# Two graph attention layers on one core: the turned probability blocks are stored and sent by query tile instead of by halves of the query quarters

## The reference

```python
h = relu(layernorm(x))
# layer 0
scores = q @ k.T / sqrt(32) + beta * adj
scores = where(adj > 0, scores, -9e15)
x = x + softmax(scores) @ v
h = relu(layernorm(x))
# layer 1
scores = q @ k.T / sqrt(384) + (adj + adj)
scores = where(any(scores != 0, axis=-1), scores, -inf)
x = x + (nan_to_num(softmax(scores)) @ v) @ Wo.T + bo
```

## Time and profile before

| what | value |
|---|---|
| median of 3 runs | 2229.5 us (2227.84 to 2229.7) |
| the profiled execution, its own time | 2227.39 us |
| its span in the profile | 2225.6 us |
| TensorE matmul busy | 1990.9 us, 89% |
| VectorE busy | 1865.0 us, 84% |
| ScalarE busy | 1643.7 us, 74% |
| GpSimd busy | 1072.6 us, 48% |
| DMA packets of the hardware queue (SyncE's) | 61.1% of 16 engines' span |
| DMA packets of the software queue (GpSimd's) | 20.6% |

### The profile page before, as it was taken

How to read it: one execution, slowest core, us unless ns; L and a number is a source line. 1 busy time by engine, 2 the same in 40 slices (tenths; PEclk the granted TensorE clock), 3 DMA queues, 4 the chain that set the end, 5 groups by cost and what they waited for, 6 DMA issues and landing times.

```text
span 2225.6 us, 52690 instructions
## 1 busy us (share of the span) xinstructions
PE 1990.9 (89%) x19584; PEld 1285.9 (58%) x19584; DVE 1865.0 (84%) x4056; ACT 1643.7 (74%) x4151; POOL 1072.6 (48%) x1541
## 2 busy tenths in 40 slices
PE   2899999999999999994499999999999999999984
PEld 1565555656555555552366666666666666666652
DVE  1999999999999999992388888888898888898881
ACT  2898888888888888882387777777777777777761
POOL 5566565565665666521433444443453434443421
PEclk8899999999999999997699999999999999999997
DMA  4688999898988888886477898888898888988784
GB/s 97 131 203 205 211 228 219 215 220 208 216 211 211 213 217 204 207 193 149 111 179 168 185 210 186 186 181 198 186 208 187 181 194 186 208 190 188 164 184 97
DMA packets 114511, 419.28 MB, mean 188 GB/s; under 512 B 35408, under 2 KB 38480, under 8 KB 114256
## 3 DMA queue, kind: packets, MB, share of 16 engines
q1 hardware_dynamic: 77392, 306.81, 61.1%
q0 software_dynamic: 36864, 109.09, 20.6%
HBM read 88.61 MB, written 25.17 MB: 51 GB/s over the span
## 4 chain that ended last, share of the span: by engine, by line
PE 35%; DVE 7%; ACT 5%; DMA 2%; issue 1%; SPq 1%; POOL 1%; DVEq 0%; POOLq 0%
PE ring L258 9%; PE sc L236 7%; PE ring L282 6%; PE out L309 6%; DVE s L374 4%; PE ring L263 3%; ACT s L503 3%; DVE pt L388 2%; PE ring L249 2%; ACT pl L521 1%; PE ring L273 1%; SPq L210 1%; DMA pk<-pt 1%; DMA bob<-in_bo 1%; PE ring L268 1%
## 5 line engine op out<-in xcount | busy, mean ns | idle before, releaser
L503 ACT ACTIVATE s<-s,nmax 128x512 f32<-128x512 f32 x1536 | 1093.6, 724 | 265.7 <-DVE nmax L374 265.2
L374 DVE CUSTOM_DVE_ANT_0 s<-sc,bias 128x512 f32<-128x512 f32 x1536 | 968.5, 686 | 123.6 <-PE sc L236 77.4
L388 DVE STREAM_TRANSPOSE pt<-s 128x2048 f32<-128x2048 f32 x288 | 663.9, 2305 | 6.3 <-issue 6.1
L236 PE MATMUL sc<-k,q 32*128 32x512 f32 x3072 | 450.0, 655 | 81.5 <-DVE nmax L374 77.6
L659 POOL TENSOR_TENSOR v<-v,bvb 128x384 f32<-128x384 f32 x128 | 130.3, 1018 | 539.4 <-ACT v L541 539.0
L309 PE MATMUL out<-pk,v 128*32 128x192 f32 x6144 | 305.8, 342 | 55.2 <-DMA pk<-pt 55.0
L503 ACT ACTIVATION_READ_ACCUMULATOR s<-s,nmax 128x1 f32 x1536 | 308.7, 201 | 0.0
L309 PEld LDWEIGHTS out<-pk,v 128*32 128x32 f32 x6144 | 186.3, 113 | 207.6 <-issue 92.3
L236 PEld LDWEIGHTS sc<-k,q 32*128 32x128 f32 x3072 | 124.6, 187 | 197.7 <-DVE nmax L374 122.3
L258 PE MATMUL ring<-hT,wq 128*128 128x512 f32 x864 | 235.8, 418 | 3.0 <-DVE hT L400 3.0
L263 PE MATMUL ring<-wv,hT 128*128 128x384 f32 x1152 | 236.4, 350 | 0.0
(11 more groups left out here) (79 smaller groups left out, 2042.0 us busy)
## 6 DMA issues: line engine op xcount, KB each, us to landing
pk<-pt SPq DMA_DIRECT2D x1536, 192.0 KB, 6.0
bias<-in_adj POOLq DMA_DIRECT2D x128, 192.0 KB, 6.5
xin<-in_x POOLq DMA_DIRECT2D x64, 192.0 KB, 6.4
res<-in_x POOLq DMA_DIRECT2D x64, 192.0 KB, 9.3
x_between<-res POOLq DMA_DIRECT2D x64, 192.0 KB, 6.6
xin<-x_between POOLq DMA_DIRECT2D x64, 192.0 KB, 6.7
res<-x_between POOLq DMA_DIRECT2D x64, 192.0 KB, 5.5
out_x<-res POOLq DMA_DIRECT2D x64, 192.0 KB, 5.4
```

Of the source, the lines that this page charges most:

```text
L236: mm = nc.tensor.matmul(m.sc[:, j, :], m.q[rows, at, P * t:P * (t + 1)], by_number(k) if t < TURNS else k, start=True, stop=True)
L374: nc.vector.tensor_tensor_reduce(out=m.s[:, t % 2, :, j, :], in0=m.sc[:, j, :].rearrange("p (n e) -> p n e", e=P), in1=m.bias[par][:, t, : ...
L388: nc.vector.transpose(out=to, in_=m.s[:, t % 2].rearrange("p a j (i e) -> p (a j i) e", e=HD)).then_inc(turned, 1)
L503: nc.scalar.activation(tile, tile, ACT.Exp, bias=m.nmax[at][:, t, j:j + 1], scale=-1.0, accum_out=m.sums[at][:, t, j:j + 1]).then_inc(exp_ ...
```

## The change

The two halves are no longer bands of partitions but sets of query tiles: `GROUPS = ((0, 1), (2,))`. `pt` and `pk` become one tensor for each group. `move` sends group 0 (tiles 0 and 1) after the second turn of the step and group 1 (tile 2) after the third. Each group has its own 16 DMAs, of 4096 bytes a partition (128 KB) in group 0 and of 2048 bytes (64 KB) in group 1. So a step has 32 DMAs in place of 16, with the same bytes. Part 1 of `pv` reads group 0 (256 columns a matmul in place of 192) and part 2 reads group 1 (128 columns). The place of each part on TensorE stays.

```diff
-HALVES = 2
-PARTS = 1 + HALVES
+GROUPS = ((0, 1), (2,))
+PARTS = 1 + len(GROUPS)
...
-        moved = [[sem(f"moved_{c}_{half}") for half in range(HALVES)] for c in range(DT)]
+        moved = [[sem(f"moved_{c}_{n}") for n in range(len(GROUPS))] for c in range(DT)]
...
-        LOADS, ADJ, MOVES = 16 * QUADS, 32 * QUADS, 16 * QUADS * QUADS // HALVES
+        LOADS, ADJ, MOVES = 16 * QUADS, 32 * QUADS, 16 * QUADS * QUADS
...
                 s = DT * b + c
-                sp.wait_ge(turned, TURNS * (s + 1))
-                for a in range(QUADS):
-                    half = a * HALVES // QUADS
-                    if a * HALVES % QUADS == 0 and not (part == "first" and c == 0):
-                        sp.wait_ge(pv_ready, PARTS * (s - 1) + half + 2)
-                    for to in range(QUADS):
-                        sp.dma_start(m.pk[HD * to:HD * (to + 1), a], m.pt[HD * a:HD * (a + 1), slab(par, c), to]).then_inc(moved[c][half], 16)
+                for n, tiles in enumerate(GROUPS):
+                    sp.wait_ge(turned, TURNS * s + tiles[-1] + 1)
+                    if not (part == "first" and c == 0):
+                        sp.wait_ge(pv_ready, PARTS * (s - 1) + n + 2)
+                    for a in range(QUADS):
+                        for to in range(QUADS):
+                            sp.dma_start(m.pk[n][HD * to:HD * (to + 1), a], m.pt[n][HD * a:HD * (a + 1), slab(par, c), to]).then_inc(moved[c][n], 16)
...
-                    quads = slice(QUADS // HALVES * (part - 1), QUADS // HALVES * part)
+                    tiles, pk = GROUPS[part - 1], m.pk[part - 1]
...
-                            to = to.rearrange("p (t a e) -> p t a e", a=QUADS, e=HD)[:, 0:TURNS, quads]
-                            p = m.pk[:, quads, j].rearrange("p a (i t e) -> p i t a e", i=QUADS, e=HD)[:, n]
+                            to = to.rearrange("p (t a e) -> p t a e", a=QUADS, e=HD)[:, tiles[0]:tiles[-1] + 1]
+                            p = pk[:, :, j].rearrange("p a (i t e) -> p i t a e", i=QUADS, e=HD)[:, n]
...
-                to = m.pt[:, slab(par, c)].rearrange("p a j (i t e) -> p (a j i) t e", i=QUADS, e=HD)[:, :, t, :]
+                n = [t in tiles for tiles in GROUPS].index(True)
+                to = m.pt[n][:, slab(par, c)].rearrange("p a j (i t e) -> p (a j i) t e", i=QUADS, e=HD)[:, :, t - GROUPS[n][0], :]
...
-        self.pt = sb("pt", [P, 2, QUADS, HC, QUADS * TURNS * HD])
-        self.pk, self.pl = sb("pk", [P, QUADS, HC, QUADS * TURNS * HD]), sb("pl", [P, HC, N])
+        self.pt = [sb(f"pt{n}", [P, 2, QUADS, HC, QUADS * len(tiles) * HD]) for n, tiles in enumerate(GROUPS)]
+        self.pk = [sb(f"pk{n}", [P, QUADS, HC, QUADS * len(tiles) * HD]) for n, tiles in enumerate(GROUPS)]
+        self.pl = sb("pl", [P, HC, N])
```

More of the change, by code:

```diff
@@ L345, in _ @@
                 if kind == "post" and i == 0:
-                    pv(B, -1, DT - 2, HALVES, B % 2, False)
+                    pv(B, -1, DT - 2, len(GROUPS), B % 2, False)
                     for n in range(PARTS):
@@ L383, in turn @@
                     d2, a2 = chunk_ahead(c, -2)
-                    for half in range(HALVES):
-                        dve.wait_ge(moved[a2][half], MOVES * (b + d2 + 1))
+                    for n in range(len(GROUPS)):
+                        dve.wait_ge(moved[a2][n], MOVES * (b + d2 + 1))
                 dve.wait_ge(exp_done, UNITS * s + HC * (t + 1))
-                to = m.pt[:, slab(par, c)].rearrange("p a j (i t e) -> p (a j i) t e", i=QUADS, e=HD)[:, :, t, :]
+                n = [t in tiles for tiles in GROUPS].index(True)
+                to = m.pt[n][:, slab(par, c)].rearrange("p a j (i t e) -> p (a j i) t e", i=QUADS, e=HD)[:, :, t - GROUPS[n][0], :]
                 nc.vector.transpose(out=to, in_=m.s[:, t % 2].rearrange("p a j (i e) -> p (a j i) e", e=HD)).then_inc(turned, 1)
@@ L831, in __init__ @@
         self.s = sb("s", [P, 2, QUADS, HC, P])
-        self.pt = sb("pt", [P, 2, QUADS, HC, QUADS * TURNS * HD])
-        self.pk, self.pl = sb("pk", [P, QUADS, HC, QUADS * TURNS * HD]), sb("pl", [P, HC, N])
-        self.wraw = [self.pt[:, 0, i].rearrange("p a (b n) -> p (a b) n", b=1)[:, 0:DT, :] for i in range(3)]
+        self.pt = [sb(f"pt{n}", [P, 2, QUADS, HC, QUADS * len(tiles) * HD]) for n, tiles in enumerate(GROUPS)]
+        self.pk = [sb(f"pk{n}", [P, QUADS, HC, QUADS * len(tiles) * HD]) for n, tiles in enumerate(GROUPS)]
+        self.pl = sb("pl", [P, HC, N])
+        self.wraw = [self.pt[0][:, 0].rearrange("p a j n -> p (a j n)")[:, DT * D * i:DT * D * (i + 1)].rearrange("p (t n) -> p t n", t=DT) for i in range(3)]
         self.nmax = [sb(f"nmax{i}", [P, NT, HC]) for i in range(2)]
```

## The result

The changed kernel takes 2405.18 us (median of 4 runs, 2397.41 to 2408.16), the kernel before 2228.67 us (its median has 4 runs here): ratio 1.0787, with a 95% interval of 1.076 to 1.0815. The ratios come from all the runs of both kernels, so they can differ a little from the quotient of two medians. The profiled execution of the changed kernel took 2406.66 us at a span of 2404.9 us, 179.3 us more than the span before. It is slower, as forecast, and inside the range, but by 176 us where 109 were forecast.

The account below looks back on a forecast made before the run. SyncE's DMA issues were to bound layer 0: +100 us there and +10 us in layer 1, with the other terms at nothing, on the profiled 2227.4 us gave about 2338 us; range 2245 to 2520 us.

Parts of the forecast that it names:

- SyncE becomes the bound of layer 0, at a floor of 0.63 us whatever the size: SyncE's issues: 32 DMAs at 0.63 us take 20.2 us a step, against layer 0's step of 19.97 us.
- the room that it started from: SyncE's queue before the change: waits of 682 us in all, read as 7.1 us of room in each of 96 steps.
- Rival 1: SyncE's issues: small DMAs cost less, 0.55 us each, and the earlier start pays; about 2200 us, chance 0.08.
- rival 3: SyncE's moves: 0.94 us a DMA whatever its bytes, 30.1 us a step; about 3060 us, chance 0.06.
- Contention 1.9 us a step: SyncE's DMAs beside GpSimd's transfer bursts: 1.9 us added a step, making SyncE's step 22.1 us.
- New waits: Group 1's waits on SyncE for the third turn and the earlier part 2: over when SyncE comes to them.
- Layer 1 nearly unchanged, +10 us: Layer 1's steps: SyncE's 22.1 us stays below 22.46 us, so bursts cost only 10 us in all.
- The pair of parts costs what it did, so nothing: TensorE's `pv`: matmuls of 256 and 128 columns take 66 + 34 = 100 ns, as two of 192 did.
- Group 0 starts earlier, worth nothing: Group 0's move needs two turns, not three, so can start about 5 us earlier: nothing, at best -16 us.
- Rival 4: GpSimd's bursts are paid nearly in full in both layers: +306 us, about 2535 us, chance 0.14.

Follow-up runs that it names:

- 24 DMAs: Changed kernel without the moves of blocks whose source and destination band are the same, except in each layer's first step: 2214.89 us, ratio 0.9952.
- the partner: Kernel before without the moves of same-band blocks, except in each layer's first step, so 12 DMAs a step: 2180.56 us, ratio 0.9801.

## Why the prediction was right, and where it was off

- *SyncE becomes the bound of layer 0, at a floor of 0.63 us whatever the size.* Right: 591 to 593 ns in the median over DMAs of 128, 96, 64 and 32 KB, and half the bytes leave the layer 0 step at 21.65 us. Only the room that it started from was misread: 4.9 us a step in layer 0, as above, and 15.0 + 7.1 us could not have fitted a step of 19.97. The sum did not use it. That initiating a DMA is usually small beside the DMA itself (the Trainium skill, "DMA: Bandwidth & Descriptors", "Issuing engines are not separate DMA queues") does not hold here for the time in which the bytes are carried: 0.59 us to issue, 0.31 us to carry 64 KB, an estimate from the 209 GB/s of the earlier trace rows. Beside the time to landing, 2.7 us in the median, the issue is short, but landings overlap and issues don't. Rival 1 is out by this, and rival 3 by the 10.06 us for 16.
- *Contention 1.9 us a step.* The term was too small as a whole, and too large for what it named. Beside GpSimd's packets SyncE lost 1.3 us a step in layer 0 and 1.6 in layer 1. But 0.8 us beside instruction fetches had no term, and 0.5 to 0.6 us of SyncE's own waits had been put at nothing (*New waits*), since both events were to lie before SyncE comes to them; that held only most of the time. The fetches stood in the trace before, as 28 us in layer 0 of longer issues beside packets of the queue q8, and SyncE's waits hid them. Together 2.7 us in place of 1.9: over 47 steps +38 us, which is layer 0's miss of 37. The time came out at the top of the forecast's own range of 2255 to 2410 us, which allowed up to 2.9 us a step here.
- *Layer 1 nearly unchanged, +10 us.* Mis-sized: +32 us. The forecast set SyncE at 22.1 us there; it took 20.3 + 1.6 + 0.8 + 0.5 = 23.2 us, more than the step's 22.46. Some 0.3 us of the growth would have come without SyncE, by the next point.
- *The pair of parts costs what it did, so nothing.* The price was right (3.01 us for the pair at the full clock), the step from it was not: a part 0.42 us longer in quarter-step 2 costs 0.3 us a step in layer 1 where SyncE isn't the bound, and the shorter one in quarter-step 0 returns nothing. The sum of an engine's busy time hides this. Nor had the prediction a term for TensorE's clock, which fell with the waits in layer 0 (0.97 to 0.93).
- *Outside the steps.* 10.8 us had no term. Presumably the last moves of a layer have nothing behind which to hide.
- *Group 0 starts earlier, worth nothing.* Right, since SyncE can't start it: for the group 0 that begins at 622.82 the second turn had ended at 610.5. With 24 DMAs, where it could, no gain showed beside the partner.
- *Rival 4 (24.5 us a step in both layers)* is out: neither layer came to it.

**Left open.** Why swapped groups lose less to contention (48.5 and 43 us beside GpSimd's packets in place of 63 and 76) is not known. Some of it may be where the 64 KB DMAs fall against the bursts; no run tested that. In the changed kernel 109 us of what is lost beside GpSimd's packets fall on the 128 KB DMAs and 35 us on the 64 KB ones; with the groups swapped it is 42 and 55 us. In both it is the first group of a step that loses more, so the size alone doesn't decide it.

## What to carry to other kernels

Before a transfer is cut into more pieces, multiply the pieces by the issue time of a short one (here 0.63 us on SyncE) and hold the product against the loop's period, with clearly more than a tenth of room on top, because fetches, contention and gated waits take the rest: at 17.7 us of issues a 19.97 us step became 21.1, at 20.3 us it became 22.9. A queue that waits 5 us a step isn't idle for nothing, it is what absorbs bursts. And when work is moved between places of an engine's order, price it at the place: a longer piece where the engine is the bound isn't paid back by a shorter one where it isn't.

## What the runs showed of the hardware that was not expected

- An instruction fetch of 16 KB (queue q8) lies beside single stretched issues of SyncE's DMAs, 45 and 53 of them in the two layers of the changed kernel, 0.8 to 0.9 us longer each in the mean. That the fetch causes them is inferred from their standing side by side.
- Cutting GpSimd's loads from 109 to 42 MB changed SyncE's excess beside its packets by 10 us of 63 in layer 0 and 18 of 76 in layer 1.
- Two loads of 1 MB and 0.8 MB that GpSimd issues one after the other: with the second two quarter-steps later, some 10 us, the kernel before is 0.8% faster and TensorE's two queues wait 68 us less for `pk` in layer 0.
- TensorE's waits for `pk` cost more than their length: during one of 7.33 us the granted clock fell to 0.50, and the `pv` part behind it took 3.64 us in place of 1.93.
